# A graph layer's selected sums merged as three bfloat16 parts instead of float32, with the work list drawn up anew

## What is computed

```python
def _layernorm(x): ...            # over the 256 features, no weights

def gnn(features, src, dst, w, W, b):
    msgs = features[src] * w[:, None]
    agg = jax.ops.segment_sum(msgs, dst, num_segments=3125, indices_are_sorted=True)
    return jnp.einsum('ni,oi->no', agg, W) + b

x = x + gnn(_layernorm(x), src, dst, edge_weight, W, b)
x = x + ffn(_layernorm(x)[None], ...)[0]   # shared MLP 256-256-128-256 + 4 experts 256-128-64-256,
                                           # gates softmax(x @ gW + gb), the best 2 of 4 weighted
```

## Time and profile before

| | us |
|---|---|
| median of 3 runs | 402.69 (402.50 to 402.74) |
| the profiled execution | 399.85 |
| its span, first to last instruction | 397.8 |
| busy: TensorE, weight loads | 358.7, 283.6 |
| busy: VectorE, ScalarE, GpSimd | 278.8, 201.6, 281.3 |

### The profile page before, as it was taken

One profiled execution on the slowest core, in us unless ns is written; L12 is line 12 of the kernel. 1 busy time (PEld: TensorE's weight loads), 2 busy tenths in 40 slices (PEclk: granted clock), 3 DMA queues, 4 the chain that ended last, 5 costly groups with the idle time before them and its releaser, 6 DMA issues.

```text
span 397.8 us, 8069 instructions
## 1 busy us (share of the span) xinstructions
PE 358.7 (90%) x2327; PEld 283.6 (71%) x2327; DVE 278.8 (70%) x1199; ACT 201.6 (51%) x553; POOL 281.3 (71%) x294
## 2 busy tenths in 40 slices
PE   4997769969899998869999999999999999998884
PEld 3885557747687877557887877877788677766672
DVE  6698999597489999460299999770249853659671
ACT  2566797466059979300079798322019521134241
POOL 7777777777777778777777777777777777777000
PEclk9999599999999999989999999999999999999999
DMA  6999649844444463534333434343433344334000
GB/s 201 376 334 308 155 103 318 206 95 105 108 113 108 105 135 83 122 109 130 108 105 108 129 99 133 96 130 105 133 103 103 101 133 129 109 107 132 28 15 25
DMA packets 53586, 53.16 MB, mean 134 GB/s; under 512 B 32507, under 2 KB 43493, under 8 KB 53413
## 3 DMA queue, kind: packets, MB, share of 16 engines
q0 software_dynamic: 13536, 36.98, 32.1%
q1 hardware_dynamic: 35220, 10.53, 11.5%
q10 hardware_dynamic: 4784, 5.11, 3.6%
HBM read 46.11 MB, written 6.48 MB: 132 GB/s over the span
## 4 chain that ended last, share of the span: by engine, by line
PE 47%; SPq 30%; issue 10%; DVE 8%; DMA 2%; ACT 1%; DVEq 0%; ACTq 0%
SPq L740 23%; PE agg_ps L1221 14%; PE hid_ps L1253 10%; PE window_ps L1154 4%; PE tok_ps L1302 4%; SPq L735 4%; PE agg_ps L1190 3%; PE tok_ps L1300 2%; PE hid_ps L1266 2%; PE hid_ps L1262 2%; DVE high_node L1621 2%; SPq L734 2%; DVE gate_x L1679 1%; DMA x_sb<-in_x 1%; PE agg_ps L1208 1%
## 5 line engine op out<-in xcount | busy, mean ns | idle before, releaser
L833 POOL DMA_INDIRECT rows<-normalised_rows,src_all x246 | 243.3, 989 | 75.0 <-issue 75.0
L1221 PE MATMUL agg_ps<-xn_all,dense 128*128 128x256 f32 x350 | 84.3, 389 | 0.0
L1253 PE MATMUL hid_ps<-xt,pack 128*128 128x256 f32 (+2 forms) x336 | 70.9, 357 | 3.1 <-ACT xt L988 3.1
L1221 PEld LDWEIGHTS agg_ps<-xn_all,dense 128*128 128x128 f32 x350 | 65.3, 193 | 11.4 <-issue 3.1
L1253 PEld LDWEIGHTS hid_ps<-xt,pack 128*128 128x128 f32 x336 | 56.1, 190 | 13.7 <-issue 7.8
L919 ACT ACTIVATE low_1h<-iota,lo_f 128x128 f32<-128x128 f32 x182 | 57.6, 394 | 0.4 <-ACT xn_all L905 0.4
L1621 DVE TENSOR_SCALAR high_node<-iota,hi_f,own_w 128x125 f32<-128x125 f32 x182 | 49.8, 363 | 0.2
L1007 ACT ACTIVATE h<-hid_ps,pack 128x256 f32<-128x256 f32 (+2 forms) x84 | 32.7, 440 | 27.5 <-PE hid_ps L1253 27.3
L817 POOL DMA_INDIRECT rows<-in_x,src_first x36 | 35.6, 988 | 11.1 <-issue 10.4
L1679 DVE CUSTOM_DVE_ANT_0 gate_x<-xn,shared 128x256 f32<-128x256 f32 x100 | 41.7, 478 | 0.1
L950 ACT ACTIVATE windows<-window_ps 128x256 f32<-128x256 f32 (+1 forms) x24 | 9.1, 378 | 64.3 <-PE window_ps L1154 64.3
(11 more groups left out here) (171 smaller groups left out, 518.7 us busy)
## 6 DMA issues: line engine op xcount, KB each, us to landing
rows<-normalised_rows,src_all POOLq DMA_INDIRECT x246
x_sb<-in_x SPq DMA_DIRECT2D x6, 512.0 KB, 10.6
normalised_rows<-xn_all ACTq DMA_DIRECT2D x6, 512.0 KB
records<-in_rec SPq DMA_DIRECT2D x184, 1.5 KB, 1.9
out<-y SPq DMA_DIRECT2D x10, 256.0 KB
pack<-in_packed SPq DMA_DIRECT2D x1, 1540.5 KB, 9.5
dense<-in_x_cols ACTq DMA_DIRECT2D x3, 512.0 KB, 8.9
x_sb<-in_x SPq DMA_DIRECT2D x3, 256.0 KB, 10.7
```

The lines of the kernel that those rows point to most:

```text
L833: pool.indirect_dma_start(rows[:, b % RING * BATCH + pos, :], None, table[:, :], bass.IndirectOffsetOnAxis(ap=src_all[:, c:c + 1], axis=0) ...
L1221: last = pe.matmul(dense_ps[0:r, t * D:(t + 1) * D], dense[:, h, t * P:t * P + r], xn_all[:, h, :], start=(h == 0 and t == 0), stop=(h == ...
L1253: last = pe.matmul(by_half(u.hid_ps[b % 2])[:, m % 2, 0:tok], w, u.xt[:, k, 0:tok], start=(k == 0), stop=(k == KD - 1))
```

## The change

The sums of a batch are no longer kept as float32. ScalarE's copy of them out of PSUM now writes bfloat16 (the first third). VectorE subtracts it from the sums in PSUM, writes the rest as bfloat16 (the second third), and subtracts that from the rest (the last third). The merge multiplies a placement that is now bfloat16 too by the three parts, one after another, into the same PSUM sums. Raw batches keep their first float32 copy, in the space of `h2`, and their product is split in the same way. TensorE's next batch waits for VectorE's first subtraction (`s_rest`). The cast of `owner` moves to the start of VectorE's stream, since its float32 space serves as `third_rest`. The planner gets a step "thirds", a merge estimate of 0.34 us instead of 0.45 us, other ranks, five open units and another order of units.

```diff
-UNIT_ORDER = "G0 D0 G1 G2 D1 G3 G4 G5 D2 G6 G7 G8 D3 G9"
-RANKS = {"open": 3, "near": 0.07, "behind": 0.36, "dve_behind": 0.94, "act_behind": 0.23, "hurry": 1.58,
+UNIT_ORDER = "D0 G0 G1 G2 D1 G3 G4 G5 D2 G6 G7 D3 G8 G9"
+RANKS = {"thirds": -2.32, "open": 5, "near": 0, "behind": 0.15, "dve_behind": 1.13, "act_behind": 0.16,
...
-            first = [("pe", "merge", sum(0.45 * len(b) for _, b in merges_of(u)),
+            first = [("pe", "merge", sum(0.34 * len(b) for _, b in merges_of(u)),
...
+            i = nxt["thirds"]
+            if i < N_BATCHES:
+                offer(at("rawout", i) if i < RAW_BATCHES else at("windows", i), RANKS["thirds"], ("thirds", i), 1.25)
...
-        windows = sb("windows", [P, KEEP, D])
-        place = sb("place", [P, KEEP, PAIR])
+        thirds = sb("thirds", [P, KEEP, PARTS, D], BF16)
+        place = sb("place", [P, KEEP, PAIR], BF16)
...
+        windows = u.h2
+        third_rest = owner_f[:, :, :].rearrange("p e n -> p (e n)")
...
+                if b < RAW_BATCHES:
+                    act.activation(windows[0:full, b, :], window_ps[0:full, 0:D], ACT.Copy).then_inc(s_windows, 1)
+                    return
                 if b >= KEEP:
                     act.wait_ge(s_merged, 1 + max(unit.i for unit in users_of(b - KEEP)))
-                act.activation(windows[0:full, b % KEEP, :], window_ps[0:full, 0:D],
-                               ACT.Copy).then_inc(s_windows, 1)
+                act.activation(thirds[0:full, b % KEEP, 0, :], window_ps[0:full, 0:D],
+                               ACT.Copy).then_inc(s_first_third, 1)
...
-                act.activation(windows[:, b % KEEP, :], u.tok_ps[:, D:2 * D], ACT.Copy).then_inc(s_raw_out, 1)
+                act.activation(thirds[:, b, 0, :], u.tok_ps[:, D:2 * D], ACT.Copy).then_inc(s_raw_out, 1)
...
+                        if q == 0:
+                            act.wait_ge(s_raw_turned, RAW_BATCHES)
                         relu2(q)
...
-                    pe.wait_ge(s_windows, b)
+                    pe.wait_ge(s_windows, min(b, RAW_BATCHES))
+                if b > RAW_BATCHES:
+                    pe.wait_ge(s_rest, 2 * b - 1)
...
-                pe.wait_ge(s_windows, mine[-1] + 1)
+                pe.wait_ge(s_thirds, mine[-1] + 1)
                 pe.wait_ge(s_place, mine[-1] + 1)
...
-                        last = pe.matmul(sums_of(unit)[:, t * D:(t + 1) * D],
-                                         place[0:full, b % KEEP, at:at + P],
-                                         windows[0:full, b % KEEP, :],
-                                         start=(b == batches[0]), stop=(b == batches[-1]))
+                        for j in range(PARTS):
+                            last = pe.matmul(sums_of(unit)[:, t * D:(t + 1) * D],
+                                             place[0:full, b % KEEP, at:at + P],
+                                             thirds[0:full, b % KEEP, j, :],
+                                             start=(b == batches[0] and j == 0),
+                                             stop=(b == batches[-1] and j == PARTS - 1))
...
+            def other_thirds(b):
+                full = P if batch_size(b) == BATCH else SLOT * len(quad(b, 0))
+                total = u.tok_ps[:, D:2 * D] if b < RAW_BATCHES else window_ps[0:full, 0:D]
+                part = [thirds[0:full, b % KEEP, j, :] for j in range(PARTS)]
+                if b == 0:
+                    dve.wait_ge(s_ruler, 2)
+                if b:
+                    dve.wait_ge(s_thirds, b)
+                dve.wait_ge(s_raw_out if b < RAW_BATCHES else s_first_third,
+                            b + 1 if b < RAW_BATCHES else b - RAW_BATCHES + 1)
+                dve.tensor_tensor(third_rest[0:full, :], total, part[0], ALU.subtract).then_inc(s_rest, 1)
+                dve.wait_ge(s_rest, 2 * b + 1)
+                dve.tensor_copy(part[1], third_rest[0:full, :]).then_inc(s_rest, 1)
+                dve.wait_ge(s_rest, 2 * b + 2)
+                dve.tensor_tensor(part[2], third_rest[0:full, :], part[1], ALU.subtract).then_inc(s_thirds, 1)
...
-                dve.wait_ge(s_const, 8)
-                dve.tensor_copy(owner[:, :, :], owner_f[:, :, :])
...
+            dve.wait_ge(s_const, 8)
+            dve.tensor_copy(owner[:, :, :], owner_f[:, :, :]).then_inc(s_ruler, 1)
             split_records(0)
```

More of the change, by code:

```diff
@@ L165 @@
 STATS_BEHIND = 3
-UNIT_ORDER = "G0 D0 G1 G2 D1 G3 G4 G5 D2 G6 G7 G8 D3 G9"
-RANKS = {"open": 3, "near": 0.07, "behind": 0.36, "dve_behind": 0.94, "act_behind": 0.23, "hurry": 1.58,
[L171 to L176, removed]
+UNIT_ORDER = "D0 G0 G1 G2 D1 G3 G4 G5 D2 G6 G7 D3 G8 G9"
+RANKS = {"thirds": -2.32, "open": 5, "near": 0, "behind": 0.15, "dve_behind": 1.13, "act_behind": 0.16,
+         "hurry": 1.88, "batch": -5.14, "rawturn": 1.22, "rawlin": -16.73, "merge": 1.57,
+         "windows": 6.06, "built": 4.11, "rowstd": -2.41, "rawxt": 6.7, "rawout": 3.22, "low": 7.15,
+         "select": -2.83, "select_late": 7.76, "place": 9.64, "records": -4.15, "onehot": 0.34,
+         "rowstats": 3.27, "rowshifts": -1.87}
+BUILD_RANKS = (12.6, 3.5, -15.35, -14.11)
+MULT_RANKS = (2.57, 1.41, 15.22, 1.74)
 GATHER_US = 1.275
@@ L198, in schedule @@
            "records": 1, "mult": 0, "load": FORE, "store": 0, "rowstats": 1, "rowstd": 1, "rowshifts": 1,
-           "rawturn": 0, "rawxt": 0, "rawlin": 0, "rawout": 0}
+           "rawturn": 0, "rawxt": 0, "rawlin": 0, "rawout": 0, "thirds": 0}
     mults = [(v, n) for v in range(len(DENSE)) for n in range(len(products_of(v)))]
@@ L222, in placed @@
     def placed(batches):
-        raw = [at("rawout", b) for b in batches if b < RAW_BATCHES]
-        return needs(at("windows", batches[-1]), *raw)
+        return at("thirds", batches[-1])
     def needs(*times):
@@ L271, in unit_steps @@
             ("pe", "l2", 2.06 * half, lambda: needs(of("h1"))),
-            ("act", "h2", 1.15 * half + 0.1, lambda: needs(of("l2"), prior("l3", one))),
+            ("act", "h2", 1.15 * half + 0.1,
+             lambda: needs(of("l2"), prior("l3", one) if q else at("rawturn", RAW_BATCHES - 1))),
             ("pe", "tgt", 0.12 * T, lambda: needs(of("mix"))),
@@ L275, in unit_steps @@
             ("pe", "spr", 0.05 + 0.22 * half, lambda: needs(of("turned"), prior("finish", one),
-                                                            at("rawout", RAW_BATCHES - 1))),
+                                                            at("thirds", RAW_BATCHES - 1))),
             ("dve", "weigh", 0.2 + 0.5 * half, lambda: needs(of("spr"), of("h2"))),
@@ L294, in fixed @@
                 row = land(b) and land(b) + 2.8
-                offer(needs(at("select", b), row, at("windows", b - 1) if b else 0.0), RANKS["batch"], ("batch", b), 0.124 * batch_size(b))
+                offer(needs(at("select", b), row, (at("windows", b - 1) if b <= RAW_BATCHES else at("thirds", b - 1)) if b else 0.0), RANKS["batch"], ("batch", b), 0.124 * batch_size(b))
             if k < len(GROUPS):
@@ L306, in fixed @@
             if r < RAW_BATCHES:
-                offer(needs(at("windows", r), at("rawout", r - 1) if r else 0.0), RANKS["rawturn"], ("rawturn", r), 0.3)
+                offer(needs(at("windows", r), at("thirds", r - 1) if r else 0.0), RANKS["rawturn"], ("rawturn", r), 0.3)
             r = nxt["rawlin"]
@@ L632, in build @@
         s_begin = sem("s_begin")
+        s_first_third = sem("s_first_third")
+        s_rest = sem("s_rest")
+        s_thirds = sem("s_thirds")
         s_begin_i = sem("s_begin_i")
@@ L1287, in spread @@
                 if q == 0 and in_order:
-                    pe.wait_ge(s_raw_out, RAW_BATCHES)
+                    pe.wait_ge(s_rest, 2 * RAW_BATCHES - 1)
                 for k in range(2):
@@ L1618, in onehots @@
                     dve.wait_ge(s_built, k - RING + 1)
-                dve.wait_ge(s_keys, block_of(v, g) + 1)
+                dve.wait_ge(s_keys, 2 * block_of(v, g) + 2)
                 for j in range(n):
@@ L1835, in _ @@
                         placement(q)
+                    elif name == "thirds":
+                        other_thirds(q)
                     elif name == "records":
```

11 lines of the change are left out of this document (4 added, 7 removed).

## The result

| | before | after |
|---|---|---|
| median, same chip | 402.72 (402.50 to 403.10, 4 runs) | 428.76 (426.18 to 432.36, 4 runs) |
| profiled execution, span | 399.85, 397.8 | 426.18, 424.1 |
| busy: TensorE, VectorE, GpSimd | 358.7, 278.8, 281.3 | 355.4, 303.1, 278.7 |
| last gather ends | 368.07 | 393.91 |
| from there to the end | 29.7 | 30.2 |

The ratio is 1.0666, with 95% [1.0616, 1.0716]. The forecast was 401.5 us, in 399.4 to 405.5: wrong in sign and size. In what follows medians are of all runs of a kernel, and ratios with their 95% intervals are of the runs within 1.5% of its fastest, which for g2 (one run of 398.55 us) are only six of twelve. Of the 26.3 us of the span, 25.8 us lie ahead of the last gather's end and 0.5 us behind it, so the question is what stopped the gathers.

A forecast was written before the change was run, and what follows sets the result against it. The gathers were taken as a floor of 368.07 us, with a 29.7 us tail. Terms: +0.9 (gathers) +1.2 (thirds) -0.5 (merge) -2.8 (backlog) = -1.2 us, from 402.69 to 401.5 us; range 399.4 to 405.5 us.

The forecast's parts named there:

- The list: Order of units, D0 before G0, D3 before G8, five open: the exchange itself gives nothing.
- rival 2: VectorE becomes the bound in mid run: +3.8 us, 406.5 us; decided by TensorE idling over 21.0 us in 60-370 us; chance 0.15.
- The floor: GpSimd's 282 gathers, about 1.29 us each, never stop for a buffer and set a floor of 368.07 us.
- Merges: On TensorE, 138 bfloat16 products replace 46 float32 ones: 4.0 us saved, of which 0.5 us in G9's own merge.
- The thirds: Three new VectorE instructions a batch, 0.42, 0.285 and 0.42 us: 28 us in all, +1.2 us in G9's chain.
- The gather stream: 24 more VectorE casts lengthen GpSimd's gathers by 36 ns each: +0.9 us on the floor.
- Rival 3: Port lock of VectorE casts against GpSimd, half or full: 3.4 to 6.8 us, 404.0 to 407.4 us; chance 0.07.
- The backlog: In the tail G9 waits 3.5 us behind other units' work; saved TensorE work removes four fifths: -2.8 us.
- Rival 4: TensorE idles around batch 23 or the merge, its clock falls to 1.2 GHz: some 1.6 us lost, 403.1 us; chance 0.09.

The follow-up runs named there:

- g2: g1 with G9's merge ahead of the second part of G8's layer 1 on TensorE, and G9's xn ahead of G8's mix_t on VectorE: 404.54 us.
- e1: The changed kernel with only D0's bias moved back in VectorE's list, to just before G0's bias: 404.92 us, ratio 1.0050 to the kernel before.
- e4: The kernel before, own list, plus one bare VectorE wait for the bias row and shifted rows of x behind records 1: 420.18 us.
- e5: The changed kernel, but SyncE sends the shared row and rows of x ahead of record blocks 2 and 3 and the weights: 412.70 us.
- e2: The changed kernel's thirds and merges with the unit order, ranks and three open units of the kernel before: 408.17 us, ratio 1.0101.
- h1: g1 with batch 2's steps also moved earlier on VectorE, ScalarE and TensorE: 404.83 us, ratio 1.0067 to the kernel before.
- g1: e1 with batch 1's steps moved ahead of one-hots and products on VectorE, ScalarE and TensorE: 404.64 us, ratio 1.0070 to the kernel before.
- p2: e1 with four more subtractions from PSUM, into a spare tile, on VectorE in every batch: 420.55 us.

## Why the prediction was wrong, point by point

- **The list** is the step that failed. The prediction weighed D0 and G0 by what their layers cost, asked only of relu2 and the raw turns whether D0 first is harmless, and called the exchange worth nothing by itself. It did not follow the first step of D0, its bias, to where it stands in VectorE's list, nor to its releaser, a load that SyncE issues at 60 us. In its place stand 24.7 us of a waiting VectorE, 28.7 us of a waiting GpSimd and 25.8 us of the span (e1 takes it away, e4 makes most of it by the wait alone, e5 scales it). No rival had it, though rival 2 named the trace of it, TensorE waiting for high_node. The signs were in what could be read: the planner's list gives the order, the planner takes a dense unit's bias as ready at 0.0, and the kernel before has the same loads at 60.7 us on SyncE.
- **The floor** was read rightly and used wrongly. Gathers do set 368 us, but "they never stop for a buffer" held for the list of before. Batch 1 was through TensorE at 60.8 us, and the gather that needs its slot is due at 64.7 us (93.39 - 28.65): 4 us of room, where the change delays batch 1 by 33: 24.7 us by the wait and the rest, which e1 shows by itself, by the other steps ahead of it.
- **Merges**: right. 138 bfloat16 products at a median of 273 ns of modelled length pass in a chain of twelve in 1.5 us, where the prediction had 1.4; the weight loads stay hidden. TensorE's busy time falls by 3.3 us, where it had 4.0.
- **The thirds**: right in size. 0.42, 0.29 and 0.43 us each; VectorE goes from 278.8 to 303.1 us, 24 us instead of 28. In G9's chain they take 1.2 us (398.26 to 399.44), as predicted.
- **The gather stream**, +0.9 us: mis-sized, nothing of it can be measured. The mean gather was 979 ns in after, 981 in e1 and 986 with 96 more casts, against 989 before. Rival 3 falls with it.
- **The backlog**, -2.8 us: mis-sized, it is 0 too. Batch 23 starts 0.85 us sooner, the merge waits 0.9 us longer, and xn and layer 1 stand as before. The prediction took TensorE's 4 us for a shift of all of the tail. g2 shows why reordering doesn't mend it: the work of G8 has to be done before the end as well. Without this term and the gathers' the sum is 402.69 + 1.2 - 0.5 = 403.4 us; the mended kernels measure 404.5 to 404.9. The forecast of a faster kernel stood on this term, so it would have failed without the stall too.
- **Rival 2** does not explain the 26 us: e2 has all of the thirds and not the stall. A small share of it stays open. By the prediction's own mark, TensorE's idle time between 60 and 370 us, the limit was 21.0 us; e1 has 21.2, h1 21.8, e2 22.4 and g1 18.8. With five times the first subtraction it costs much (p2), and at the start of the kernel it holds at any load: VectorE works 34 of 40 us there, and what is moved ahead delays the rest (h1).
- **Rival 4**: the clock did fall, to 0.55 to 0.59, but behind the stall of TensorE; in the tail it was 0.98.

## What to carry to other kernels

When a change brings a new static order, don't price the order by its sums: list what has moved ahead on each in-order engine, find the releaser of each such step (a DMA on another queue above all) and the time at which it came in the old trace. A step that never waited shows nothing in the old profile, and costs all that is queued behind it once it stands too early. A plan that was fitted to one set of costs is part of the change: the same thirds came with 1.0% more under one set of ranks and 1.5% less under another, and correcting one number of the planner gave a third list, 5.6% slower than before.

## What the runs showed of the hardware that was not expected

- **Single long gathers.** In 12 of 14 profiled kernels one to three of the 246 gathers took 2.0 to 4.3 us instead of 0.95, nine of them between 216 and 233 us into the span, as in p2:

```profile
232.95 3.97 POOL L845 DMA_INDIRECT rows<-normalised_rows,src_all  x1 [0.30 <-issue]
```

  In after and e1 there was none. Each holds up the gathers behind it, so they may be part of the 1 to 2% by which single executions of one kernel differ here (before: 398.8 to 407.2 us in 23 runs); with one profile of each kernel that is not shown. Their cause wasn't tried and stays open.
- **A wait on one engine passes on whole.** Between e1 and after, 24.7 us more on VectorE made 24.2 us more on GpSimd (28.65 instead of 4.48): the 4 us of room between them had gone to other steps.
